# Constant rows of the shift set by GpSimd instead of VectorE, and an exponential on ScalarE ahead of the first score

## The chip, the core and the metric

The kernel runs on one core of a Trainium2 chip. The core has five engines with instruction streams of their own: TensorE (PE in the profile), VectorE (DVE), ScalarE (ACT), GpSimd (POOL) and SyncE (SP), which here does nothing but issue DMA transfers. They share an on-chip memory of 128 partitions (SBUF); TensorE writes its products into a second one (PSUM). Engines meet only at semaphores: an instruction adds to one when it is done, and another engine waits until it has a value. The metric is the device time of one execution in microseconds (us).

## What is computed

One transformer layer on a sequence of 2048 rows of 128 numbers, with 16 heads of width 64 and 8 experts of width 352 of which each row uses 2, beside a shared one:

```python
x = x + attention(layernorm(x), qkv_w, qkv_b, out_w, out_b)
    # logits = q k^T / 8, causal mask, softmax, times v, times out_w
x = x + ffn(layernorm(x), gate_w, expert_*, shared_*)
    # shared: (silu(x Wg) * (x Wu)) Wd; routed: softmax of 8 logits, top 2,
    # their weights made to sum to 1, each expert the same form
```

## The kernel before, in words

**Blocks and heads.** The 2048 rows are NB = 4 blocks of 512, or NT = 16 tiles of 128. For each of the 16 heads the scores are computed transposed (keys on partitions, queries along the row) in NG = 20 groups of two key tiles by one block of queries. A group is two score products on TensorE (`scores`, L1308 and L1309), masks for diagonal tiles (L1321), two exponentials on ScalarE (`exps`: L719 writes the value in 32 bits, L720 in 16), a subtraction on GpSimd that gives the low part (`p_low`, L585), and the product with v (`p_times_v`, L1340 to L1344), which runs LAG = 3 groups later. There are two score buffers (STRING = 2), so group n + 2 waits for the exponentials of group n.

**The shift.** Softmax needs the maximum of each query row. The maxima of a head are worked out one head ahead, by products on TensorE (L1233) that VectorE reduces (L1024 on the diagonal, L1028 elsewhere). They are negated, turned (L1238), split in two 16-bit parts divided by 16384 (L1037, L1040) and laid by DMA (L471, L476) into rows D and D + 1, that is 64 and 65, of `q_lo_shift`. The second score product, L1309, has 66 rows: rows 64 and 65 of `k_hi_one` hold the constant SHIFT_UNIT = 16384 in all 2048 columns, so that it adds the shift to every score. These constant rows, one pair for each of the two sets of buffers, are written once. Before, VectorE does it with its first two instructions (L1084), and TensorE waits for `one_rows` ahead of its first score.

**The opening.** SyncE issues x in four transfers (L417, one block each, into `attn`), then the weights. For each block VectorE takes statistics of the rows (L796, L800), ScalarE the square root of the variance (L641), VectorE the reciprocal and the normalised rows (L806, L809), TensorE turns them (L1205), ScalarE writes the 16-bit high part (L646) and VectorE the low part (L815). Then come the products for q and k of head 0 (L1198 to L1200, named `qk`), split by ScalarE (L674) and VectorE (L1009), those for v (L1223, L680, L1018), and the first maxima. The order of all of that on each engine is written out by hand in `first_norm` and the lists PROLOGUE and SLOTS. ScalarE also rounds the first weights (L705) when they have landed, and GpSimd takes the remainder (`split_pair_weights`, L544), which the first q and k product needs (`w_lo_ready`).

**GpSimd at the start** makes the constants: the identity, `eps`, the masks (L531, L534, which count `masks_ready` to 2), the columns of ones beside v (L537), the start value of the maxima (L538) and a row of whole numbers (L539). Of these, those that count `consts` are waited for by ScalarE ahead of its first exponential, and by TensorE and VectorE ahead of the first masked maximum.

**ScalarE's tables.** A function such as the square root or the exponential needs its table, which an ACT_TABLE_LOAD brings in. Copies run in either. The loads are put into the stream ahead of the first instruction that needs another table. The kernel calls a square root on one number at its start (L723), whose result nothing uses.

Of the kernel before, what the change touches and what calls it, by code (L numbers as in the profile page):

```python
# [14 lines left out]
ALU, ACT = mybir.AluOpType, mybir.ActivationFunctionType  # L15
# [7 lines left out]
H, D = 16, 64  # L23
# [9 lines left out]
SHIFT_UNIT = 16384.0  # L33
# [142 lines left out]
def layer_kernel(nc, x_t, x_rows_in, qkv_w, qk_bias_in, v_bias, out_w, out_bias, gate_w_t, ffn_w, out_rows):  # L176
    ctx = ExitStack()
    with ctx:
        def sb(name, shape, dtype):
            return ctx.enter_context(nc.sbuf_tensor(name, shape, dtype))  # L180
# [4 lines left out]
        def sem(name):  # L185
            return ctx.enter_context(nc.semaphore(name))
# [6 lines left out]
        def part(k):  # L193
            return qk_parts[:, k * T:(k + 1) * T]
# [8 lines left out]
        q_lo_shift, k_hi_one = [part(2), part(6)], [part(3), part(7)]  # L203
# [9 lines left out]
        std = sb("std", [P, NT], F32)  # L213
# [18 lines left out]
        eps = sb("eps", [P, 1], F32)  # L232
# [98 lines left out]
        consts, pool_self, masks_ready = sem("consts"), sem("pool_self"), sem("masks_ready")  # L331
        one_rows = sem("one_rows")
# [1 line left out]
        bias_sum_ready, res_bias_ready = sem("bias_sum_ready"), sem("res_bias_ready")  # L334
        x_stats, x_mean_var, ln_std, ln_rstd = sem("x_stats"), sem("x_mean_var"), sem("ln_std"), sem("ln_rstd")
        x_normalised, x_turned, xn_ready = sem("x_normalised"), sem("x_turned"), sem("xn_ready")
        sqrt_warm = sem("sqrt_warm")
        xn_hi_ready, xn_lo_ready = sem("xn_hi_ready"), sem("xn_lo_ready")
        res_ready = sem("res_ready")
        st_ready, exp_done = sem("st_ready"), sem("exp_done")  # L340
# [39 lines left out]
        def blk(b):  # L380
            return slice(b * BLK, (b + 1) * BLK)
# [139 lines left out]
        def _(pool):  # L521
# [11 lines left out]
                                    pattern=[[-1, P]], channel_multiplier=1).then_inc(masks_ready, 1)  # L533
            nc.gpsimd.affine_select(out=mask_cols[:], in_=mask_cols[:], compare_op=ALU.is_ge, fill=NEG, base=0,  # L534
                                    pattern=[[1, P]], channel_multiplier=-1).then_inc(masks_ready, 1)
            for s in range(2):
                nc.gpsimd.memset(v_parts[s][:, :, :, D:D + 1], 1.0).then_inc(consts, 1)  # L537
            nc.gpsimd.memset(row_max[:], -1.0e9).then_inc(consts, 1)  # L538
# [54 lines left out]
            for h in range(H):  # L593
                i, s = divmod(h, 2)
# [41 lines left out]
        def _(act):  # L636

            def first_norm():
                def deviation(b):
                    act.wait_ge(x_mean_var, b + 1)  # L640
                    nc.scalar.activation(std[:, 4 * b:4 * b + 4], mean_var[:, 4 * b:4 * b + 4, 1], ACT.Sqrt, bias=eps[:]  # L641
                                         ).then_inc(ln_std, 1)

                def high_part(b):
                    act.wait_ge(x_turned, b + 1)
                    nc.scalar.copy(xn_hi[:, blk(b)], turn_bank[b]).then_inc(xn_hi_ready, 1)  # L646

                def whole(b):
                    act.wait_ge(xn_lo_ready, b + 1)
                    nc.scalar.copy(xn[:, blk(b)], turn_bank[b]).then_inc(xn_ready, 1)  # L650

                deviation(0)
                deviation(1)
                split_pair_weights(0)
                high_part(0)
                deviation(2)
                high_part(1)
                deviation(3)
                qk_high(0)
                high_part(2)  # L660
                qk_high(1)
                high_part(3)
                qk_high(2)
                for b in range(NB):
                    whole(b)
                    if b == 0:
                        qk_high(3)
                split_out_weights(0)
                for q in range(4):
                    v_high(q)  # L670
            def qk_high(b):
                act.wait_ge(bg_ready, drained(("qk", 0, b)))
                act.wait_ge(w_landed[0], 32)
                nc.scalar.activation(k_lohi[0][:, blk(b)], bg[:, NUMBER["qk", 0, b] % BGRING, :], ACT.Identity,  # L674
                                     bias=qk_bias[0][:, 0:1]).then_inc(qk_hi_ready, 1)

            def v_high(q):
                act.wait_ge(bg_ready, drained(("v", 0, q)))
                bank = bg[:, NUMBER["v", 0, q] % BGRING, :]
                nc.scalar.copy(v_quad(0, q, 0, D), bank.rearrange("p (t h c) -> p h t c", t=4, h=2)).then_inc(v_hi_ready, 1)  # L680
# [22 lines left out]
            def split_pair_weights(i):  # L703
                act.wait_ge(w_landed[i % 2], (i // 2 + 1) * 32)
                nc.scalar.copy(w_hi[i % 2], w_raw[i % 2][:, :, 0:2 * D]).then_inc(w_hi_ready, 1)  # L705

            def split_out_weights(i):
                act.wait_ge(wo_landed, 32)
                nc.scalar.copy(wo_hi[i % 2], wo_all[:, i, :]).then_inc(wo_hi_ready, 1)
# [17 lines left out]
            act.wait_ge(masks_ready, 2)  # L727
            nc.scalar.copy(mask_cols_b[:], mask_cols[:]).then_inc(consts, 1)
            first_norm()
            act.wait_ge(consts, N_CONST + 2)  # L730
            for h in range(H):
                i, s = divmod(h, 2)
# [59 lines left out]
        def _(dve):  # L792
# [25 lines left out]
            def first_norm():  # L818
                x_statistics(0)
                x_statistics(1)  # L820
                normal(0)
                x_statistics(2)
                normal(1)
                low_part(0)
                x_statistics(3)
                normal(2)
                low_part(1)
                normal(3)
                low_part(2)
                low_part(3)  # L830
# [249 lines left out]
                nc.vector.tensor_tensor(attn[:, 4 * b:4 * b + 4, s * D:(s + 1) * D], pv4[:, :, 0:D],  # L1080
                                        rden[:, B % 2].broadcast_to([P, 4, D]), ALU.mult).then_inc(attn_ready, 1)

            for s in range(2):
                nc.vector.memset(k_hi_one[s][D:D + 2, :], SHIFT_UNIT).then_inc(one_rows, 1)  # L1084
            first_norm()
            for task in PROLOGUE[0:8]:
                background_task(task)
# [479 lines left out]
```

## Time and profile before

| | us |
|---|---|
| median of three runs | 918.85 (917.88 to 920.42) |
| the profiled execution, device time | 918.86 |
| its span | 917.1 |
| TensorE busy | 853.2 (93%) |
| ScalarE, VectorE, GpSimd busy | 684.9, 695.6, 710.7 |
| mean granted TensorE clock | 0.974 |

Around the span there are 918.86 - 917.1 = 1.8 us that the profile doesn't divide. A line such as `41.10 0.60 PE L1308 MATMUL st<-qk_parts ... [1.89 <-ACT p_parts L720]` reads: starts 41.10 us after the span's start, takes 0.60 us, on TensorE, line 1308 of the kernel, writes `st` from `qk_parts`; TensorE had been idle for 1.89 us until the ScalarE instruction of line 720 that writes `p_parts` ended. Buffers are shown by the tensor's name, so `k_hi_one` and `q_lo_shift`, which are pieces of `qk_parts`, carry that name; x lands in `attn`, the rounded weights are `split`, and the normalised rows stand in `prob`.

### The profile page before, as it was taken

How to read it: one execution, taken by the hardware profiler on the slowest of the kernel's cores; microseconds unless marked ns; L12 is line 12 of the kernel's file. 1: busy time of each engine (PE TensorE's matmuls, PEld its weight loads, DVE VectorE, ACT ScalarE, POOL GpSimd, SP SyncE). 2: the span in 40 equal slices, each digit the busy share in tenths (PEclk: the TensorE clock that was granted, in tenths of full speed). 3: DMA queues.
4: the chain of work that ended last, by engine and by line, in shares of the span. 5: the costliest groups of instructions: out<-in, count | busy, mean ns of one | idle time of the engine just before them, and what ended most of it. 6: DMA issues, size and time to landing. Idle time of an engine off the chain costs nothing.

```text
span 917.1 us, 25699 instructions
## 1 busy us (share of the span) xinstructions
PE 853.2 (93%) x10266; PEld 577.4 (63%) x10266; DVE 695.6 (76%) x1771; ACT 684.9 (75%) x842; POOL 710.7 (77%) x448
## 2 busy tenths in 40 slices
PE   4788999999999999999999999999999787969997
PEld 2345666666666666666666666666666563538886
DVE  7798797888879797989797979787976455445444
ACT  4366888988898889898989898988889782124442
POOL 1466889999999899889989898988889877254442
PEclk9799999999999999999999999999999999779998
DMA  6121232323242424233301020202020001112214
GB/s 181 24 52 65 56 67 65 68 55 68 64 74 50 79 55 86 64 69 73 62 17 42 16 48 1 58 2 48 2 48 3 2 2 44 40 39 69 62 44 145
DMA packets 60149, 48.33 MB, mean 53 GB/s; under 512 B 8688, under 2 KB 57714, under 8 KB 59904
## 3 DMA queue, kind: packets, MB, share of 16 engines
q1 hardware_dynamic: 57760, 42.48, 20.7%
q0 software_dynamic: 2272, 4.22, 1.3%
q8 instruction: 83, 1.36, 0.6%
q14 instruction: 34, 0.28, 0.1%
HBM read 13.93 MB, written 16.29 MB: 33 GB/s over the span
## 4 chain that ended last, share of the span: by engine, by line
PE 60%; DVE 25%; issue 5%; POOL 4%; ACT 3%; DMA 2%; SPq 1%; POOLq 0%; DVEq 0%; ACTq 0%
DVE row_max L1028 10%; PE st L1308 7%; PE st L1309 7%; PE bg L1233 7%; PE pv L1340 5%; PE pv L1342 4%; PE pv L1344 4%; POOL p_parts L585 4%; DVE junk L1024 3%; PE bg L1483 3%; PE bg L1223 3%; PE bg L1200 2%; PE bg L1198 2%; PE bg L1199 2%; DVE att_parts L1050 2%
## 5 line engine op out<-in xcount | busy, mean ns | idle before, releaser
L585 POOL TENSOR_TENSOR p_parts<-prob,p_parts 128x1024 f16<-128x1024 f32 x320 | 612.4, 1935 | 93.5 <-ACT p_parts L720 91.6
L719 ACT ACTIVATE prob<-st,p_bias 128x1024 f32<-128x1024 f32 x320 | 331.1, 1035 | 101.9 <-PE st L1309 72.3
L720 ACT ACTIVATE p_parts<-st,p_bias 128x1024 f16<-128x1024 f32 x320 | 330.8, 1034 | 0.0
L1028 DVE TENSOR_REDUCE row_max<-bg 128x1 f32<-128x512 f32 x384 | 250.6, 685 | 9.4 <-PE bg L1233 8.2
L1340 PE MATMUL pv<-v_parts,p_parts 128*128 128x65 f16 x2176 | 232.7, 193 | 3.2 <-POOL p_parts L585 2.6
L1342 PE MATMUL pv<-v_parts,p_parts 128*128 128x64 f16 x2176 | 233.0, 195 | 0.0
L1344 PE MATMUL pv<-v_parts,p_parts 128*128 128x65 f16 x2176 | 231.9, 192 | 0.0
L1308 PE MATMUL st<-qk_parts 128*128 128x512 f16 (+3 forms) x640 | 221.7, 349 | 7.4 <-ACT p_parts L720 4.6
L1309 PE MATMUL st<-qk_parts 66*128 66x512 f16 (+3 forms) x640 | 220.6, 351 | 0.0
L1340 PEld LDWEIGHTS pv<-v_parts,p_parts 128*128 128x128 f16 x2176 | 202.3, 96 | 28.4 <-DVE attn L1080 9.0
L1233 PE MATMUL bg<-qk_parts 128*128 128x512 f16 (+3 forms) x640 | 210.7, 353 | 9.8 <-DVE row_max L1028 2.1
L1342 PEld LDWEIGHTS pv<-v_parts,p_parts 128*128 128x128 f16 x2176 | 201.8, 97 | 16.0 <-issue 0.3
L1344 PEld LDWEIGHTS pv<-v_parts,p_parts 128*128 128x128 f16 x2176 | 202.2, 99 | 0.0
L1024 DVE CUSTOM_DVE_ANT_0 junk<-bg,mask_wide 128x128 bf16<-128x128 f32 (+3 forms) x256 | 121.7, 483 | 3.1 <-PE bg L1233 2.1
L1233 PEld LDWEIGHTS bg<-qk_parts 128*128 128x128 f16 x640 | 62.9, 98 | 77.4 <-DVE row_max L1028 13.1
L1309 PEld LDWEIGHTS st<-qk_parts 66*128 66x128 f16 x640 | 62.4, 97 | 52.6 <-issue 1.4
L1308 PEld LDWEIGHTS st<-qk_parts 128*128 128x128 f16 x640 | 62.9, 98 | 50.0 <-ACT p_parts L720 7.0
L1007 DVE TENSOR_SCALAR qk_parts<-bg,qk_bias 128x512 f16<-128x512 f32 x60 | 44.9, 749 | 53.8 <-PE bg L1200 53.6
L622 POOL DMA_INDIRECT y_dram<-p_parts,v_parts x39 | 37.8, 970 | 48.5 <-DVE p_parts L1159 39.1
L777 ACT ACTIVATE prob<-st 128x352 f32<-128x352 f32 x39 | 18.1, 463 | 49.7 <-PE st L1464 40.2
L1167 DVE TENSOR_TENSOR prob<-prob,st 128x352 f32<-128x352 f32 x39 | 20.3, 521 | 44.5 <-issue 37.9
L1009 DVE SCALAR_TENSOR_TENSOR qk_parts<-bg,qk_bias,qk_parts 128x512 f16<-128x512 f32 x64 | 47.9, 751 | 2.6 <-ACT qk_parts L674 0.5
(230 smaller groups left out, 1048.3 us busy)
## 6 DMA issues: line engine op xcount, KB each, us to landing
qk_parts<-qk_parts SPq DMA_DIRECT2D x192, 64.0 KB, 2.0
row_dram<-fill SPq DMA_DIRECT2D x8, 1290.0 KB, 10.6
qk_parts<-qk_parts SPq DMA_DIRECT2D x16, 256.0 KB, 3.0
stage_raw<-ffn_w SPq DMA_DIRECT2D x16, 176.0 KB, 2.6
v_parts<-row_dram SPq DMA_DIRECT2D x39, 64.5 KB
qk_parts<-y_dram SPq DMA_DIRECT2D x8, 256.0 KB, 4.7
w_raw<-qkv_w SPq DMA_DIRECT2D x8, 192.0 KB, 2.3
down_w<-ffn_w SPq DMA_DIRECT2D x1, 1536.0 KB, 8.1
```

Of the source, the lines that this page charges most:

```text
L585: nc.gpsimd.tensor_tensor(o, a, b, ALU.subtract).then_inc(p_lo_ready, 1)
L719: nc.scalar.activation(o32, src, ACT.Exp, bias=p_bias[:], scale=D ** -0.5)
L720: nc.scalar.activation(o16, src, ACT.Exp, bias=p_bias[:], scale=D ** -0.5).then_inc(exp_done, 1)
L1009: nc.vector.scalar_tensor_tensor(out=q_lo_shift[s][:, blk(b)], in0=bank, scalar=bias, in1=k_lohi[s][:, blk(b)], op0=ALU.add, op1=ALU.subtr ...
L1024: nc.vector.tensor_tensor_reduce(masked[k % BGRING][:, 0:width], bank[:, 0:width], mask_wide[:, BLK - width:BLK], 1.0, -3.0e38, ALU.add, A ...
L1028: nc.vector.tensor_reduce(row_max[:, t, c:c + 1], bank, AX_X, ALU.max).then_inc(bg_drained, 1)
L1233: mm = nc.tensor.matmul(bank[:, 0:width], q_hihi[s][:, tile(t)], k_lohi[s][:, c * BLK:c * BLK + width], start=True, stop=True)
L1308: nc.tensor.matmul(out, k_lohi[s][:, tile(kt)], q_hihi[s][:, q], start=True, stop=False)
L1309: mm = nc.tensor.matmul(out, k_hi_one[s][0:D + 2, tile(kt)], q_lo_shift[s][0:D + 2, q], start=False, stop=not diagonal)
L1340: nc.tensor.matmul(out, p_hi[:, n % PRING, cols], v[:, 0:D + 1], start=(kt == 0 and j == 0), stop=False, skip_group_check=True)
L1342: nc.tensor.matmul(out[:, 0:D], p_hi[:, n % PRING, cols], v[:, D + 1:VW], start=False, stop=False, skip_group_check=True)
L1344: mm = nc.tensor.matmul(out, p_lo[:, n % PRING, cols], v[:, 0:D + 1], start=False, stop=(kt == 4 * b + j), skip_group_check=True)
```

## The change

GpSimd writes the constant rows, between the masks and the columns of ones, with one wait ahead (for its own masks) and one behind; VectorE no longer does. ScalarE calls an exponential on one number, into a cell of `std` that has been read by then, when its work of the opening is issued, and waits for it ahead of its first score.

```diff
-        sqrt_warm = sem("sqrt_warm")
+        sqrt_warm, exp_warm = sem("sqrt_warm"), sem("exp_warm")
@@ gpsimd
             nc.gpsimd.affine_select(out=mask_cols[:], in_=mask_cols[:], compare_op=ALU.is_ge, fill=NEG, base=0,
                                     pattern=[[1, P]], channel_multiplier=-1).then_inc(masks_ready, 1)
+            pool.wait_ge(masks_ready, 2)
+            for s in range(2):
+                nc.gpsimd.memset(k_hi_one[s][D:D + 2, :], SHIFT_UNIT).then_inc(one_rows, 1)
+            pool.wait_ge(one_rows, 2)
             for s in range(2):
                 nc.gpsimd.memset(v_parts[s][:, :, :, D:D + 1], 1.0).then_inc(consts, 1)
@@ scalar
             first_norm()
+            nc.scalar.activation(std[:, 1:2], eps[:], ACT.Exp).then_inc(exp_warm, 1)
+            act.wait_ge(exp_warm, 1)
             act.wait_ge(consts, N_CONST + 2)
@@ vector
-            for s in range(2):
-                nc.vector.memset(k_hi_one[s][D:D + 2, :], SHIFT_UNIT).then_inc(one_rows, 1)
             first_norm()
```

On GpSimd, from the masks to the remainder of the first weights (`split`), the order before is:

```order
L534 AFFINE_SELECT mask_cols<-mask_cols 128x128
L537 MEMSET v_parts 128x32 x2
L538 MEMSET row_max 128x64
L539 IOTA iota_row 128x128
L544 TENSOR_TENSOR split<-w_raw,split 128x256
```

and after the change, whose file has other line numbers:

```order
L534 AFFINE_SELECT mask_cols<-mask_cols 128x128
L538 MEMSET qk_parts 2x2048 x2
L541 MEMSET v_parts 128x32 x2
L542 MEMSET row_max 128x64
L543 IOTA iota_row 128x128
L548 TENSOR_TENSOR split<-w_raw,split 128x256
```

Two MEMSETs of 2 partitions by 2048 numbers now stand ahead of five instructions, the last of which TensorE waits for. On ScalarE, from the last copy of the normalised rows to the second exponential of the first group, the order before is:

```order
L709 CAST split<-wo_all 128x128
L680 CAST v_parts<-bg 128x2x4x64 x4
L719 ACT_TABLE_LOAD
L719 ACTIVATE prob<-st,p_bias 128x1024
L720 ACTIVATE p_parts<-st,p_bias 128x1024
```

and after:

```order
L713 CAST split<-wo_all 128x128
L684 CAST v_parts<-bg 128x2x4x64 x4
L734 ACT_TABLE_LOAD
L734 ACTIVATE std<-eps 128x1
L723 ACTIVATE prob<-st,p_bias 128x1024
L724 ACTIVATE p_parts<-st,p_bias 128x1024
```

The table load now belongs to the exponential on one number, which waits for no other engine; the first exponential of the scores has none of its own.

## Rows read from the trace of the kernel before

**Rows 1.** The page's first line: the span.
```profile
span 917.1 us, 25699 instructions
```

**Rows 2.** The chain that ended last, in order of time: start, us, what.
```profile
1.30 1.76 DVE qk_parts L1084
...
5.24 0.88 DVE stats L796 x4
...
37.60 0.03 issue
37.63 1.28 ACT L719
38.93 1.11 ACT prob L719
...
67.90 6.72 DMA qk_parts<-shift_row
```

**Rows 3.** Issues of x, and us from issue to landing of blocks 0, 1, 2.
```profile
0.81 2.11 SPq L417 DMA_DIRECT2D attn<-x_rows_in  x4
...
DMA to landing us min/median/max: 3.0/3.0/3.0
...
DMA to landing us min/median/max: 3.3/3.3/3.3
...
DMA to landing us min/median/max: 5.1/5.1/5.1
```

**Rows 4.** VectorE in order of time, opening: start, us, instruction, xcount.
```profile
6.44 0.84 DVE L796 BATCH_NORM_STATS2 stats<-attn 128x6 f32<-128x128 f32 x4
...
7.79 1.11 DVE L809 TENSOR_SCALAR prob<-attn,mean_var,rstd 128x128 f32<-128x128 f32 x4
8.82 0.87 DVE L796 BATCH_NORM_STATS2 stats<-attn 128x6 f32<-128x128 f32 x4
...
11.23 0.68 DVE L815 TENSOR_TENSOR xn_lo<-st,xn_hi 128x512 f16<-128x512 f32 x1
```

**Rows 5.** ScalarE in order of time, opening; brackets: idle before, and its releaser.
```profile
8.68 0.40 ACT L705 CAST split<-w_raw 128x256 f16<-128x256 f32 x1 [0.65 <-DMA qk_bias<-qk_bias_in]
10.17 0.59 ACT L646 CAST xn_hi<-st 128x512 f16<-128x512 f32 x1 [1.09 <-PE st L1205]
...
37.63 1.28 ACT L719 ACT_TABLE_LOAD   x1 [11.65 <-PE st L1321]
```

**Rows 6.** GpSimd in order of time, then groups by shape (busy us, mean ns), then L537.
```profile
2.85 0.38 POOL L537 MEMSET v_parts<- 128x32 f16 x2
...
3.12 0.28 POOL L539 IOTA iota_row<- 128x128 f32 x1
9.16 0.67 POOL L544 TENSOR_TENSOR split<-w_raw,split 128x256 f16<-128x256 f32 x1 [5.76 <-ACT split L705]
...
L556 POOL TENSOR_SCALAR res<-res,res_bias 128x2048 f32<-128x2048 f32 x1 | 5.4, 5447 | 4.1 <-DVE res_bias L1090 4.1
L528 POOL MEMSET mask_wide<- 128x512 f32 x1 | 0.5, 514 | 0.0
L526 POOL MEMSET eps<- 128x1 f32 x1 | 0.1, 88 | 0.0
...
L537 POOL MEMSET v_parts<- x2: 238/281/324, 2.9 to 2.9; 128x32 f16 x2
```

**Rows 7.** TensorE and VectorE around head 0's third group; then stretch 42 to 43.
```profile
12.28 0.63 PE L1198 MATMUL bg<-xn_hi,split 128*128 128x512 f16 x1
...
41.10 0.60 PE L1308 MATMUL st<-qk_parts 128*128 128x512 f16 x1 [1.89 <-ACT p_parts L720]
...
42.59 0.69 DVE L1028 TENSOR_REDUCE row_max<-bg 128x1 f32<-128x512 f32 x1 [2.28 <-PE bg L1233]
...
44.69 0.38 PE L1233 MATMUL bg<-qk_parts 128*128 128x512 f16 x1
...
42.00:43.00 1.00, 1.00 (x4) 0.37 (x3) 0.41 (x1) 0.20 (x1) 1.00 (x1) 0.50 0.00 0
```

In the last row the numbers are: length of the stretch, busy us and count of TensorE, its weight loads, VectorE, ScalarE and GpSimd, granted clock as a share of full speed, DMA share and GB/s.

## The prediction

> **What bounds the kernel now.** I read the chain of waits in order of time first. The span is 917.1 us [rows 1], and both instructions that the change touches are links of that chain [rows 2]: it opens on VectorE with two MEMSETs of 1.76 us, the first at 1.30, runs on to the statistics of x at 5.24, and passes through ScalarE's table load, 1.28 us at 37.63, to the first exponential at 38.93. The reader is to see that these links come before everything else: the opening is one chain of short steps across VectorE, TensorE and ScalarE, with no slack of its own. Then I read the landing of x, since the statistics wait for that too; then ScalarE, GpSimd and VectorE in order of time in the first 12 us, for what would be late next; and TensorE with its granted clock around the first scores. Behind 75 us nothing changes: sixteen heads, the routing and the experts follow in the same order, so what matters is only how much earlier they begin.
>
> **Term 1, the MEMSETs leave VectorE.** The statistics of block 0 start at 5.24 [rows 2]. With the MEMSETs gone they wait for x alone. Its first transfer is issued at 0.81 and lands 3.0 us later, at 3.8 [rows 3]. Counting a landing from the start of its issue, and 0.06 us (an estimate, from gaps such as the 0.03 of issue in [rows 2]) to the waiting instruction, the statistics start at 3.87. The gain is 5.24 - 3.87 = 1.37 us, not the 3.94 us from 1.30 to 5.24: two thirds of the removed time was beside the transfer anyway.
>
> What is late next? The other blocks of x: the four issues take 2.11 us from 0.81, about 0.53 apart [rows 3]. Block 1 lands at 1.33 + 3.3 = 4.6; its statistics would start at 6.44 - 1.37 = 5.07 [rows 4]. Block 2 lands at 1.87 + 5.1 = 7.0; it is wanted at 8.82 - 1.37 = 7.45 [rows 4]. Both are there with about 0.45 us to spare. ScalarE: the rounding of the weights stands at 8.68 because the weights' bias lands then [rows 5], and this does not move. Behind it stands the high part of block 0, now at 10.17, which could start at 8.80 but gets its turn at 9.08. It ends at 9.08 + 0.59 = 9.67. VectorE takes it up at 11.23 now [rows 4], or 9.86 then, as its own work stands ahead. So the 0.28 us are hidden. I take the whole 1.37; the bounds are 0.9 (x or the weights a little late) and 1.6.
>
> **Term 2, the MEMSETs come to GpSimd.** No row shows a MEMSET of 2048 numbers there. The nearest ones are contiguous fills: 1 number 88 ns, 512 numbers 514 ns [rows 6], so 0.834 ns for each further number, and 88 + 2047 x 0.834 = 1.79 us for one, 3.6 for two, from about 2.95 (where the columns of ones start now, 2.85, and 0.1 for the wait on the masks). What stands behind them, from the columns of ones at 2.85 to the end of the row of numbers at 3.12 + 0.28 = 3.40, takes 0.55 us more, so GpSimd is free at 7.1. Its next work, the remainder of the weights, is released at 9.16 by ScalarE [rows 6]: cost 0, covered by 2.0 us of idle time. The others who wait for these constants do so after 26 us. Upper bounds: at the rate of the 128x2048 operation, 5.45 us each, GpSimd would be free at 2.95 + 10.9 + 0.55 = 14.4, the remainder done at 15.1, and the first q and k product, now at 12.28 [rows 7], would be 2.8 us late. At the rate of the 32-number fill of v_parts, (238 - 88) / 31 = 4.8 ns [rows 6], one takes 9.9 us, GpSimd is free at 23.3, the remainder done at 24.0, and the product 11.7 us late. I take 1.79, since the fill of v_parts differs in its stride and the 128x2048 row reads as well as writes.
>
> A rule speaks mildly against this half of the change. Beside the second MEMSET VectorE would begin the normalised rows (L809, at 7.79 - 1.37 = 6.4 [rows 4]). The Trainium skill (SBUF — State Buffer, Who interferes with whom) says that a VectorE tensor_scalar in a two-port mode and GpSimd lock each other out for a whole instruction. By that rule VectorE would wait until about 6.6, and the time would be 0.2 us longer; no row shows GpSimd filling beside such an instruction, and the sum goes without it.
>
> **Term 3, the table load.** ScalarE is idle for 11.65 us ahead of the load [rows 5]: it has nothing to do between the last of v's high parts, which ends at 37.63 - 11.65 = 26.0, and the first score. The load and the exponential on one number fit there with some 10 us to spare, and cost nothing. The load is removed from between the mask product and the first exponential: 38.93 - 37.63 = 1.30 us [rows 2]. TensorE's third group waits for these exponentials, with 1.89 us of idle time [rows 7], and VectorE waits 2.28 us for the product of a maximum behind that group [rows 7], so both engines move by the whole 1.30 and neither has other work that would be in the way: bounds 1.0 and 1.3. From there the chain is mostly VectorE's maxima up to 67, the end of head 0's last shift, then its transfer, which takes 6.72 us at 67.90 behind a large load of weights [rows 2]. Both are issued by SyncE in the same order and after work of VectorE, so they move with the rest.
>
> The Trainium skill (ScalarE: Activation LUTs, What ACT_TABLE_LOAD costs) puts a switch of tables at about 2.66 us, 1.28 for the load and 1.38 for a drain. The 1.28 agrees with the trace. The drain is not in it: 0.03 us of issue stand between the mask product, for which ScalarE waited, and the load, and 0.02 us between the load's end and the exponential [rows 2, 5]. By the rule the sum would be 1.38 us lower.
>
> **Sum.** 918.86 (the profiled execution) - 1.37 + 0 - 1.30 = 916.19. The median of the runs shown is 918.85, so nothing has to be converted. That is 0.29% faster; a change of 0.3% (2.8 us) is about what a measurement of this kernel can tell from none, and the three runs before span 2.5 us.
>
> **TensorE's clock** is the unknown of the opening. From 41.10 to 44.69 its products of 512 columns take 0.63 us, later 0.38 [rows 7]; the granted clock in between is 0.50 of full speed [rows 7], the lower of the two levels, 1.2 GHz. It fell after the idle time in front of 41.10 that waited for ScalarE. With the load gone this idle time is 1.89 - 1.30 = 0.6 us, and the clock may stay at 2.4 GHz. The stretch of 3.6 us at half rate would take 1.8 less, but VectorE has six maxima of up to 0.69 us there [rows 7], 3 to 4 us of work of its own, so I estimate 1.0 more gained, at most 1.8. It can go the other way too: if the clock rises at the same time after the start as now and not at the same place in the work, 1.37 us more of TensorE's work runs at half rate in the opening (12.28 is such a place, 0.63 us for 512 columns [rows 7]), and each such rise gives back up to 1.37 / 2 = 0.7 us. There is at least one more than the one at 44.69, since the clock that fell at 41 had been up.
>
> **The rivals.**
> - *Clean shift*, 916.2, give or take 0.6. For it: every wait behind the two links follows from them. Chance 0.45.
> - *The clock stays up at 41 us*, 915.2. For it: the shorter idle time. Against it: 0.6 us of it is left, and ScalarE, not TensorE, sets the pace of the next groups. Chance 0.22.
> - *Part is given back*, at the clock's rises, by the lock of the SBUF port, or by x landing late in a stretch where transfers share the engines: one of the terms halves, 917.2 to 918.0. Chance 0.22.
> - *The drain exists*, hidden from the rows: 916.19 - 1.38 = 914.8. Against it: the two gaps of 0.03 and 0.02 us [rows 2]. Chance 0.03.
> - *GpSimd's fill is slow, and the first q and k product waits for the remainder of the weights.* At the upper rate 11.7 us late instead of 1.37 early: 918.86 + 11.7 - 1.30 = 929.3. It decides where two MEMSETs hold GpSimd beyond 12.28 + 1.30 - 0.67 - 0.55 = 12.4 us, that is at over 4.7 us each, where the time is 918.86 again; at 5.45 us it is 918.86 + 2.8 - 1.3 = 920.4. For it: the shape is in no row, and GpSimd's v_parts fill is slow. Chance 0.04, with 0.04 more for a slowdown that I can't name.
>
> **How the numbers follow.** The predicted time is the clean shift's, 916.2. The limit of 0.3% is at 916.1, so half of the clean shift's chance is on either side of it. Faster by over 0.3%: 0.23 + 0.22 + 0.03 + 0.01 of the third case = 0.49. Within: 0.22 + 0.21 = 0.43. Slower: 0.08. The range of 8 in 10 leaves out the slow fill and the ends: 914.2, the clock with its upper gain, to 918.7, where nearly all is given back.
>
> **What would show it.** In the profile of the changed kernel the statistics of block 0 start at 3.9 with x's transfer as the releaser; GpSimd's two MEMSETs take 1.8 us each and its remainder of the weights still starts at about 9.2; the first q and k product is at 10.9; ScalarE has a table load at about 25 and none at the first score; the first exponential starts at 38.93 - 2.67 = 36.3, and TensorE's first product of head 0's last block, now behind the transfer that ends at 74.6 [rows 2], at about 72.0. The prediction is wrong if the MEMSETs last over 4 us, if the first exponential moves by less than 2 us, or if it moves by 2.7 us and the end does not.

## The result, and the profile after

The changed kernel took 914.50 us, median of 7 runs (912.64 to 917.08), against 918.23 us for the kernel before (7 runs, 915.92 to 920.42). The ratio is 0.9960, 95% interval 0.9942 to 0.9978: 3.7 us faster, between 2.0 and 5.3. Forecast were 2.7. On another chip the ratio was 0.9975 (0.9965 to 0.9985): 895.12 us, median of 9 runs, against 896.98, median of 17, so 2.2 us by the ratio, between 1.3 and 3.1. Both intervals hold the forecast.

The chain that ended last, in order of time (start, us, what), of the changed kernel; it answers to [rows 2]:

```profile
0.79 3.04 DMA attn<-x_rows_in
3.86 0.88 DVE stats L802 x4
...
63.99 6.66 DMA qk_parts<-shift_row
...
70.79 0.38 PE st L1312
```

The MEMSETs of VectorE are gone, and x's transfer stands in their place: the statistics start at 3.86, forecast 3.87. The transfer of head 0's last shift starts at 63.99 instead of 67.90, 3.9 us earlier, where 2.67 were forecast. VectorE in order of time in the opening, which answers to [rows 4]:

```profile
6.41 1.33 DVE L815 TENSOR_SCALAR prob<-attn,mean_var,rstd 128x128 f32<-128x128 f32 x4
7.67 0.86 DVE L802 BATCH_NORM_STATS2 stats<-attn 128x6 f32<-128x128 f32 x4
...
9.04 1.19 DVE L815 TENSOR_SCALAR prob<-attn,mean_var,rstd 128x128 f32<-128x128 f32 x4
10.15 0.68 DVE L821 TENSOR_TENSOR xn_lo<-st,xn_hi 128x512 f16<-128x512 f32 x1
```

The first four normalised rows take 1.33 us instead of 1.11, the next four 1.19 instead of 1.12. So the low part of block 0 (the last line) starts 11.23 - 10.15 = 1.08 us earlier, and not 1.37. GpSimd and then ScalarE of the same kernel; they answer to [rows 6] and [rows 5]:

```profile
2.94 3.54 POOL L538 MEMSET qk_parts<- 2x2048 f16 x2
...
8.71 0.67 POOL L548 TENSOR_TENSOR split<-w_raw,split 128x256 f16<-128x256 f32 x1 [1.62 <-ACT split L709]
```

```profile
24.43 0.60 ACT L684 CAST v_parts<-bg 128x512 f16<-128x512 f32 x1 [0.99 <-PE bg L1227]
25.04 1.28 ACT L734 ACT_TABLE_LOAD   x1
26.33 0.20 ACT L734 ACTIVATE std<-eps 128x1 f32<-128x1 f32 x1
36.65 1.11 ACT L723 ACTIVATE prob<-st,p_bias 128x1024 f32<-128x1024 f32 x1 [10.12 <-PE st L1325]
```

The two MEMSETs take 1.77 us each (forecast 1.79), and GpSimd still waits 1.62 us for ScalarE behind them. The table load stands where ScalarE has nothing else to do; 10.12 us of idle time are left behind it. The first exponential starts at 36.65 instead of 38.93, 2.28 us earlier, where 2.67 were forecast. So 0.4 us had been lost by then: some 0.29 at the normalised rows and 0.12 at the last block of x, which TensorE turned in 0.94 us before and in 1.06 us now. And between the first exponential and 64 us 3.91 - 2.28 = 1.6 us more were gained. TensorE of the changed kernel at the third group, with the granted clock (third number from the end) of three stretches; they answer to [rows 7]:

```profile
38.25 0.63 PE L1237 MATMUL bg<-qk_parts 128*128 128x512 f16 x1
38.83 0.45 PE L1312 MATMUL st<-qk_parts 128*128 128x512 f16 x1
39.12 0.38 PE L1313 MATMUL st<-qk_parts 66*128 66x512 f16 x1
```

```profile
38.00:39.00 1.00, 1.00 (x6) 0.39 (x4) 0.96 (x4) 1.00 (x2) 0.15 (x1) 0.51 0.00 0
39.00:40.00 1.00, 1.00 (x6) 0.40 (x5) 0.86 (x2) 0.93 (x2) 1.00 (x1) 1.00 0.00 0
...
42.00:43.00 1.00, 0.47 (x16) 0.35 (x12) 0.94 (x4) 1.00 (x2) 0.72 (x2) 1.00 0.00 0
```

Here the clock rises to full speed just before 39 and stays. In the profile of before it was at half from 41 to 44.7. The forecast had named that as a rival, with "at most 1.8 us". The experiments ask whether the change brought it about.

### The profile page after: what moved, and what is told of

Its sections match the earlier page's. It is cut to its first block, busy times and chain, and to the rows that moved or that the text cites. A ratio compares the mean times of both kernels' runs of the same rounds, so it can differ in the third digit from the quotient of the medians.

```text
span 912.8 us, 25700 instructions
## 1 busy us (share of the span) xinstructions
PE 851.0 (93%) x10266; PEld 576.5 (63%) x10266; DVE 692.0 (76%) x1769; ACT 685.1 (75%) x843; POOL 714.1 (78%) x450
## 4 chain that ended last, share of the span: by engine, by line
PE 59%; DVE 24%; POOL 4%; issue 4%; DMA 3%; ACT 3%; another core or an unknown queue 2%; SPq 1%; POOLq 0%; DVEq 0%; ACTq 0%
DVE row_max L1034 10%; PE st L1312 7%; PE st L1313 7%; PE bg L1237 7%; PE pv L1344 5%; PE pv L1346 5%; PE pv L1348 4%; POOL p_parts L589 4%; DVE junk L1030 3%; PE bg L1487 3%; PE bg L1227 3%; PE bg L1204 2%; PE bg L1202 2%; PE bg L1203 2%
```

## The experiments

Theory A: the two parts add up, and beside them the table load's idle time on TensorE made the clock fall, so that its going keeps the clock up. Theory B, the rival: the idle time has no part in it; the phase of the clock against the work decides, and only 2.5 us belong to the change.

The runs of this section are from three other chips, on which the kernel before takes about 897 us. A profile shows one execution; where a time is given as a ratio, it is from six to ten runs of the kernel named, against 23 (first three experiments) or 17 runs of the kernel before on the same chip. The opening is nearly the same on all: the statistics of the kernel before start at 5.24 there too.

**The MEMSETs alone moved.** The edit, against the changed kernel:

```diff
-            nc.scalar.activation(std[:, 1:2], eps[:], ACT.Exp).then_inc(exp_warm, 1)
-            act.wait_ge(exp_warm, 1)
```

> The changed kernel without its exponential on one number: only the MEMSETs move to GpSimd. Theory A (the two parts are separate, and the clock stayed up because the table load no longer makes TensorE idle): statistics of block 0 start at 3.86 instead of 5.24; the first exponential, behind its table load, starts 1.0 us earlier than before (37.9); TensorE's idle time ahead of the third group stays about 1.9 us and the clock falls there as before, so TensorE's first product of the last block of head 0 comes at about 73.8 (74.76 - 1.0) and the time is about 1.0 us under before. Theory B (the clock's phase against the start of the kernel decides, not the idle time): the clock stays up here too, and that product comes at 72.3, time 2.4 us under before.

Measured: ratio to before 1.0001 (0.9990 to 1.0012), 897.42 against 897.37 us. ScalarE and TensorE in order of time:

```profile
36.47 1.28 ACT L723 ACT_TABLE_LOAD   x1 [11.65 <-PE st L1323]
37.77 1.11 ACT L723 ACTIVATE prob<-st,p_bias 128x1024 f32<-128x1024 f32 x1
...
39.94 0.61 PE L1310 MATMUL st<-qk_parts 128*128 128x512 f16 x1 [1.89 <-ACT p_parts L724]
40.34 0.63 PE L1311 MATMUL st<-qk_parts 66*128 66x512 f16 x1
```

and of its chain that ended last:

```profile
66.78 6.72 DMA qk_parts<-shift_row
...
73.64 0.38 PE st L1310
```

The first exponential is 1.16 us earlier than in the first profile of before, the clock falls at 40 (the product of 512 columns takes 0.63), and TensorE's first product of head 0's last block came at 73.64, forecast 73.8. As to the opening this was theory A's numbers. But the time did not move: the interval reaches 0.9 us down, so that the 1.0 us expected here lies a little outside it, and the 1.37 us of the prediction's first term further.

**The exponential alone added.** The edit, against the changed kernel:

```diff
@@ gpsimd
-            pool.wait_ge(masks_ready, 2)
-            for s in range(2):
-                nc.gpsimd.memset(k_hi_one[s][D:D + 2, :], SHIFT_UNIT).then_inc(one_rows, 1)
-            pool.wait_ge(one_rows, 2)
@@ vector
+            for s in range(2):
+                nc.vector.memset(k_hi_one[s][D:D + 2, :], SHIFT_UNIT).then_inc(one_rows, 1)
             first_norm()
```

> The changed kernel with its MEMSETs back on VectorE: only the exponential on one number is added. Theory A: the statistics start at 5.24, the first exponential at 37.6 (1.30 earlier), TensorE's idle time ahead of the third group is 0.6 us, the clock does not fall there, and the first product of the last block of head 0 comes at 74.76 - 1.3 - 1.4 = 72.0; time 2.7 us under before. Theory B: the opening has its old phase, the clock falls as before; the product comes at 73.5, time 1.3 us under before.

Measured: ratio 0.9969 (0.9951 to 0.9986), 895.29 against 897.37 us. The first exponential starts at 37.80, the clock stays up from 40 on, the first product of the last block comes at 71.58 (forecast 72.0). Theory A's numbers again, and here the time agrees too (2.8 us, between 1.3 and 4.4; 2.7 expected). Theory B's 1.3 is at the edge of the interval.

**The kernel before, with TensorE kept busy in the gap.** The edit, against the kernel before, in `scores`, ahead of its first wait:

```diff
+                if h == 0 and n == 2 and k == 0:
+                    for _ in range(7):
+                        nc.tensor.matmul(pv[:, :], xn_hi[:, 0:P], xn_hi[:, blk(0)], start=True, stop=True)
```

> The kernel before with seven more products of 128x512 on TensorE (into the bank of the v products, which is free then), issued ahead of the wait of the third group of head 0, where TensorE is idle for 1.9 us; the table load stays where it was. Theory A: TensorE has no idle time there, the granted clock stays at full speed through 41 to 45, the maxima end 1.4 us earlier, and the first product of the last block comes at about 73.4, time 1.4 us under before. Theory B (idle time does not matter): the clock falls at 41 as before, the product stays at 74.7 and the time is unchanged.

Measured: ratio 0.9985 (0.9973 to 0.9996), 896.37 us, 1.3 us by the ratio, between 0.4 and 2.4 (1.4 expected). The clock stays up, the last shift's transfer starts at 66.48, 1.42 us earlier than in the first profile of before. That looked like a proof of theory A, and the next repetition took the profile's part of it away.

**The kernel before, unchanged, profiled again.** It was run beside the kernels that follow, and then three times more on another chip.

> The kernel before, profiled on the chip of this comparison, so that openings can be laid beside each other. Both theories: its opening repeats to 0.2 us (statistics 5.24, first exponential 38.9, first product of head 0's last block 74.8), since in the runs so far the opening hardly depended on the chip. If that product moves by over 0.5 us between two executions of this kernel, single looks at the opening can't tell theories apart.

Measured: the expectation fell. The statistics are at 5.24 and the first exponential at 39.04, but the product of the last block came at 72.71, 2.05 us earlier than in the first profile, over four times the 0.5 us beyond which single profiles of the opening can't tell the theories apart. TensorE in order of time at the third group, and then the chain's transfer:

```profile
39.17 0.42 PE L1321 MATMUL st<-mask_cols_b,ident_b 128*128 128x128 bf16 x2
41.22 0.39 PE L1308 MATMUL st<-qk_parts 128*128 128x512 f16 x1 [1.20 <-ACT p_parts L720]
```

```profile
66.57 6.00 DMA qk_parts<-shift_row
```

Without any edit the product behind the gap takes 0.39 us and not 0.60: the clock is up, and the transfer starts at 66.57, where the kernel with the seven fills had 66.48. So the profile with the fills had shown nothing. Its time is lower all the same: the interval doesn't hold 1. Whether the fills help in those executions in which the clock would fall is not shown.

> The kernel before, unchanged, a third profile. The question is how often TensorE's clock falls in front of the third group of head 0. So far: in the first profile of this kernel and in the one with the MEMSETs alone moved it rose at 37.4 (36.2) and fell at 41 (40); in the second profile of this kernel it rose only at about 39 and did not fall, which moved the last shift's transfer from 67.90 to 66.57. Theory A' (the table load's idle time makes a fall possible, and the phase of the clock decides whether it comes): some of these three profiles show the fall, with the transfer at 67.9, the others show none, with 66.5. Theory C (the first profile was an outlier): none does.

> The same kernel again, as the run ahead of it. Theory A': fall or none, transfer of the last shift at 67.9 or at 66.5 and nothing in between. Theory C: no fall, 66.5.

> The same kernel again, as the two runs ahead of it. Theory A': fall or none, transfer of the last shift at 67.9 or at 66.5. Theory C: no fall, 66.5.

Measured: none of the three shows a fall, which is theory C's forecast. First exponential at 39.40, 39.05 and 39.05; the transfer starts at 66.95, 66.54 and 66.35. Of five profiles of the kernel before, the first alone has it, and beside it the one with the MEMSETs alone moved. In these two the clock rose early, at about 37.7 and 36.6 by the shares of the stretches of 1 us (0.63 in 37 to 38, 0.72 in 36 to 37), and fell behind the gap. In the other four profiles of the kernel before it rose between 39.2 and 40.1 and stayed. (The expectation of the third profile put the two rises 0.3 us too early.) The two patterns part much earlier, at the products for the third block's q and k. Here is the first of them in the first and in the second profile of the kernel before:

```profile
17.34 0.38 PE L1198 MATMUL bg<-xn_hi,split 128*128 128x512 f16 x1
```

```profile
17.41 0.63 PE L1198 MATMUL bg<-xn_hi,split 128*128 128x512 f16 x1
```

The third to fifth profiles have 0.63 or 0.64 there too, and the kernel with the MEMSETs alone moved has 0.38, at 16.18. What sets the moment of the first rise no run shows.

The third profile's exponential is 0.35 us late for another reason. VectorE and then GpSimd:

```profile
7.79 1.47 DVE L809 TENSOR_SCALAR prob<-attn,mean_var,rstd 128x128 f32<-128x128 f32 x4
```

```profile
8.46 0.71 POOL L544 TENSOR_TENSOR split<-w_raw,split 128x256 f16<-128x256 f32 x1 [5.06 <-ACT split L705]
```

ScalarE rounded the weights early in this execution, at 7.97 instead of 8.68, and GpSimd's subtraction of them ran beside the normalised rows, which took 1.47 us instead of 1.11.

So the first profile is one outcome of two, and the rarer. Against the common one, 39.05 and 66.5, the kernel with the MEMSETs alone moved gains 1.28 us at the first exponential (37.77), of which 0.12 belong to the early clock, and then loses it to the clock (66.78 is no earlier than 66.5). That agrees with its ratio of 1.0001, as far as one profile can say; but ten runs were timed, and that the clock fell in most of them is not shown.

**The changed kernel again.**

> The changed kernel once more, timed in five rounds on the chip of this comparison. Theory A (two parts that add up, and the clock that stays up): first product of head 0's last block 3.9 us earlier than in the kernel before (70.8), time 3.9 us under it, ratio 0.9957. Theory B (the clock's part was luck of one execution): 2.5 us, ratio 0.9973, with the clock at half speed somewhere between 39 and 45.

> The changed kernel, a third profile. In its two profiles so far the clock rose at 38.2 to 38.8 and stayed up, with the transfer at 64.0 and 64.1. Theory A': with 0.6 us of idle time no fall comes whatever the phase, transfer at 64.0 again. Theory C says the same. If it falls here, the transfer is at about 65.4 and the change has no bearing on the clock.

Measured, the first of them timed: ratio 0.9975 (0.9965 to 0.9985). ScalarE's first exponential and the chain's transfer:

```profile
36.63 1.11 ACT L723 ACTIVATE prob<-st,p_bias 128x1024 f32<-128x1024 f32 x1 [10.17 <-PE st L1325]
```

```profile
64.07 6.77 DMA qk_parts<-shift_row
```

Against the profile of the kernel before on the same chip that is 39.04 - 36.63 = 2.41 us at the exponential and 66.57 - 64.07 = 2.50 at the transfer's start. The 2.2 us of the timing (1.3 to 3.1) agree with that and not with theory A's 3.9. It is theory B's forecast of 2.5 that came out, though not by its mechanism, since the clock was never at half between 39 and 45. The forecasts were for TensorE's first product of the last block, though, and that starts at 70.98 against 72.71, 1.73 us earlier and not 2.5: the transfer ahead of it took 6.77 us here and 6.00 there. The third profile started its first exponential at 37.60 and the transfer at 65.05, 1.0 us later than the other two. TensorE in order of time shows where most of the difference arose:

```profile
18.95 0.58 PE L1202 MATMUL bg<-xn_hi,split 128*128 128x512 f16 x1 [0.87 <-DVE qk_parts L1015]
19.33 0.63 PE L1203 MATMUL bg<-xn_lo,split 128*128 128x512 f16 x1
19.75 0.63 PE L1204 MATMUL bg<-xn_hi,split 128*128 128x512 f16 x1
```

These are the products for the last block's q and k; in the other two profiles each took 0.38 us. TensorE reached full speed later in the work, and by the end of v's products it was 25.11 - 24.15 = 0.96 us behind. Of that, 0.33 us had been there ahead of these products: the normalised rows of block 1 took 1.45 us instead of 1.11, beside GpSimd's subtraction (8.97 to 9.64), and VectorE's last low part starts at 17.45 instead of 17.12. The clock's share is 0.6.

Behind the transfer this profile shows something that none of the theories has. The granted clock is at half again, from about 73.6 for 3.4 us. First a stretch of it and the eight products for v of that time, then the same products in the second profile of the changed kernel:

```profile
74.00:75.00 1.00, 1.00 (x18) 0.94 (x17) 1.00 (x4) 1.00 (x2) 0.00 (x0) 0.50 0.00 0
...
75.38 1.90 PE L1227 MATMUL bg<-w_raw,xn 128*128 128x128 f32 x8
```

```profile
73.54 1.13 PE L1227 MATMUL bg<-w_raw,xn 128*128 128x128 f32 x8
```

VectorE's next scaling of the products with v by the row sums (L1086, in the kernel before L1080) starts at 82.94, against 80.33 and 80.15 in the other two profiles, and 82.06 to 82.78 in the last four profiles of the kernel before: at this point nothing is left of the gain. The kernel with the MEMSETs late, below, shows the same (73.6, scaling at 82.81). The last such scaling, at the end of head 15, starts at 757.39 and 758.25 in the second and third profiles of the changed kernel and at 758.96 to 759.49 in those four, 0.7 to 2.1 us later.

**The MEMSETs three times.** The edit, against the changed kernel:

```diff
-            for s in range(2):
-                nc.gpsimd.memset(k_hi_one[s][D:D + 2, :], SHIFT_UNIT).then_inc(one_rows, 1)
-            pool.wait_ge(one_rows, 2)
+            for k in range(6):
+                if k > 1:
+                    pool.wait_ge(one_rows, k - 1)
+                nc.gpsimd.memset(k_hi_one[k % 2][D:D + 2, :], SHIFT_UNIT).then_inc(one_rows, 1)
+            pool.wait_ge(one_rows, 6)
```

with TensorE's wait for `one_rows` raised to 6.

> The changed kernel with each constant-row MEMSET issued three times on GpSimd (six of 1.77 us, from 2.9 to about 13.9 with the waits between them). GpSimd's remainder of the first weights then starts at about 14.4 instead of 8.7 and ends at 15.1. If it is covered by idle time only up to the first q and k product, as predicted, that product starts at 15.1 instead of 11.2, and everything behind it, the first exponential too, is 3.9 us later than in the changed kernel (40.5). Rival (other work hides part of it): less than 2 us later.

Measured: VectorE, GpSimd and TensorE in order of time:

```profile
2.95 10.96 POOL L540 MEMSET qk_parts<- 2x2048 f16 x6
...
6.35 3.93 DVE L817 TENSOR_SCALAR prob<-attn,mean_var,rstd 128x128 f32<-128x128 f32 x4
...
11.56 2.50 DVE L817 TENSOR_SCALAR prob<-attn,mean_var,rstd 128x128 f32<-128x128 f32 x4
14.52 0.66 POOL L550 TENSOR_TENSOR split<-w_raw,split 128x256 f16<-128x256 f32 x1
15.33 0.58 PE L1204 MATMUL bg<-xn_hi,split 128*128 128x512 f16 x1
```

The remainder of the weights starts at 14.52 and the product at 15.33; forecast were 14.4 and 15.1. The first exponential came at 40.16, 3.5 us later than in the changed kernel, 3.9 forecast. So the point from which the MEMSETs delay the first product is where the prediction had put it. But there is a second effect that it had left out of the sum: VectorE's four normalised rows take 3.93 us instead of 1.11 beside the fills, and the next four 2.50. The statistics between them (0.85 for four) are not lengthened at all. One kind of VectorE instruction stands still while GpSimd fills, the other runs on. The chain that ended last goes over this second effect and not over the first product:

```profile
11.56 2.50 DVE prob L817 x4
14.06 0.59 DVE xn_lo L823
```

VectorE's low part of block 0 starts at 13.98, 3.83 us later than in the changed kernel, and the product 4.13 us later. The two are so close that this run doesn't show what the delayed product alone would have cost. One time only was taken, 899.03 us.

**The MEMSETs late.** The edit, against the changed kernel: the MEMSETs and their waits move from behind the masks to

```diff
             split_out_weights(0)
+            pool.wait_ge(wo_lo_ready, 1)
+            for s in range(2):
+                nc.gpsimd.memset(k_hi_one[s][D:D + 2, :], SHIFT_UNIT).then_inc(one_rows, 1)
+            pool.wait_ge(one_rows, 2)
             pool.wait_ge(res_bias_ready, 1)
```

> The changed kernel with its two MEMSETs on GpSimd behind the remainder of the first output weights, in the idle time between 22.4 and 26.4, where VectorE works from the other memory. If GpSimd's fill holds back VectorE's normalised rows (the first tensor_scalar took 760 ns beside it, 347 before), the first four now take 1.11 us instead of 1.33 and the first exponential comes 0.2 to 0.3 us earlier than in the changed kernel (36.4); time 0.3 us less, which the timing can't tell. Rival: the lengthening came from x's transfers, and the four stay at 1.33. A risk: the fill ends at 26.0 and the addition to the residual starts at 26.4, so nothing is late.

Measured: ratio 0.9970 (0.9959 to 0.9981), 894.92 us, beside 0.9975 of the changed kernel: no difference that can be told. VectorE and GpSimd:

```profile
6.49 1.11 DVE L815 TENSOR_SCALAR prob<-attn,mean_var,rstd 128x128 f32<-128x128 f32 x4
...
8.69 0.67 POOL L544 TENSOR_TENSOR split<-w_raw,split 128x256 f16<-128x256 f32 x1 [5.29 <-ACT split L709]
...
8.90 1.30 DVE L815 TENSOR_SCALAR prob<-attn,mean_var,rstd 128x128 f32<-128x128 f32 x4
```

The first four are back at 1.11, so it was GpSimd's work that lengthened them, the fills or the short constants that had been behind them, and not x's transfers. The next four now take 1.30: they meet GpSimd's remainder of the weights, from 8.69 to 9.36, which in the first profile of the kernel before lay between two such groups. So the low part starts at 10.13, no earlier than the changed kernel's 10.07 and 10.15. The first exponential came at 37.31, not at 36.4, for the same reason as in the changed kernel's third profile: the last q and k products were at half rate. The 0.2 us that the edit gives at the first rows are smaller than what the subtraction and the clock do by themselves.

**The MEMSETs late, and TensorE kept at work.** The edit, against the kernel just told of, with two more products of 128x512 ahead of the third group:

```diff
             pe.wait_ge(ones_ready, 1)
+            for _ in range(20):
+                nc.tensor.transpose(pv[:, 0:P], ident[:], ident[:])
             turn_normal(0)
...
-            for task in PROLOGUE[8:]:
+            for k, task in enumerate(PROLOGUE[8:]):
+                if k == 3:
+                    pe.wait_ge(res_bias_ready, 1)
                 background_task(task)
+                if k >= 3:
+                    nc.tensor.matmul(pv[:, :], xn_hi[:, 0:P], xn_hi[:, blk(0)], start=True, stop=True)
...
-            pe.wait_ge(res_bias_ready, 1)
```

> The previous kernel (MEMSETs late) with idle TensorE kept at work in the opening: 20 turns of the identity before the first normalised rows, one product of 128x512 behind each maximum of the prologue from the fourth on, and two ahead of the third group, all into the bank of the v products. If the clock is the other lever of the opening, granted clock 1.0 from about 10 to 45, products of 512 columns at 0.38 us throughout, the first exponential about 2 us earlier than without (34.4), and 1 more us by the end of the first maxima of the next groups; time 2.5 to 3 us under the changed kernel, ratio to before 0.993. Rival: the opening is bound by VectorE, and the fills gain under 1 us.

Measured: ratio 0.9962 (0.9950 to 0.9975), 894.19 us. TensorE, then ScalarE's first exponential and the chain's transfer:

```profile
10.88 0.63 PE L1202 MATMUL bg<-xn_hi,split 128*128 128x512 f16 x1
...
18.37 0.38 PE L1202 MATMUL bg<-xn_hi,split 128*128 128x512 f16 x1 [0.87 <-DVE qk_parts L1015]
...
33.20 0.38 PE L1315 MATMUL st<-qk_parts 128*128 128x512 f16 x1
...
34.85 1.11 ACT L723 ACTIVATE prob<-st,p_bias 128x1024 f32<-128x1024 f32 x1 [8.64 <-PE st L1328]
```

```profile
62.26 6.50 DMA qk_parts<-shift_row
```

The 20 turns at the start had no effect: the products from 10.88 to 17 still took 0.63 us. The fills between the maxima did: the first scores, from 33.20, take 0.38 where they took 0.63 in the changed kernel, and the first exponential comes at 34.85 (34.4 expected), 1.8 us earlier than the changed kernel's 36.63. The transfer starts 1.8 us earlier too. But the median is only 0.9 us under the changed kernel's, where 2.5 to 3 were expected, and the intervals of the two ratios overlap, so that this version has the lowest ratio but is not clearly the fastest. The same profile shows where part of the gain went: the clock is at half from 69.2 for 3.4 us, the first product of the last block takes 0.56 us instead of 0.38, and the next scaling (L1086) starts at 79.71, only 0.62 us ahead of the changed kernel's 80.33.

## Why the prediction was right, and where it was not

- **The MEMSETs leave VectorE.** Right in the profiles: 5.24 became 3.86 by the row; x's transfer is what ends the wait; blocks 1 and 2 were in time. Not shown in the time: the MEMSETs alone moved gave a ratio of 1.0001, and the 1.37 us of this term lie outside its interval.
- **The MEMSETs come to GpSimd at no cost.** Their size (1.77 for 1.79) and their cover (GpSimd idle behind them) were right. The cost was not zero: they hold VectorE's normalised rows back by 0.19 to 0.27 us. The prediction had set this aside as a rule of the Trainium skill (SBUF — State Buffer, Who interferes with whom) that no row showed. The traces agree with the rule and its 0.2 us: in the four profiles with the MEMSETs there these rows start at 6.37 to 6.45 and all end at 7.74 or 7.75, as if all had begun at about 6.6; beside six fills they take 3.93 us, with the fills elsewhere 1.11. By the same section a VectorE instruction with one input outside the two-port modes is free of it, and the statistics were.
- **The weights.** The prediction took it that ScalarE's rounding stands at 8.68 and does not move. It starts between 7.97 and 8.68 in the five profiles of the kernel before, and where GpSimd's subtraction behind it meets normalised rows, these take longer, by 0.07 us (first profile of the changed kernel, block 1) to 0.36 us (third profile of the kernel before, block 0). So this cost comes without the change too; by its earlier rows the change only moves where it can fall.
- **The table load.** Right. In the kernel with the exponential alone added, the first exponential came at 37.80 against 39.04 to 39.05 in three of the five profiles of before, 1.25 us; the load's row is 1.28. No drain was seen: the load starts 0.01 us after a copy has ended and the exponential on one number 0.01 us after the load. The 2.66 us that the Trainium skill gives (ScalarE: Activation LUTs, What ACT_TABLE_LOAD costs) are not what a switch takes here.
- **The sum.** 2.67 forecast; 2.41 at the first exponential and 2.50 at the transfer by two profiles of one chip, 2.2 (1.3 to 3.1) by its timing. Of the 0.26 missing at the exponential 0.19 is the hold-up of the normalised rows beside GpSimd. At the product behind the transfer the same two profiles have 1.73. So the sum is good to 0.4 us at the first exponential in two profiles, and 1.2 us off in the third; the two halves add up there (1.16 without the early clock, and 1.25, against 2.41) but are not told apart by the times (the MEMSETs alone moved: between 1.1 us slower and 0.9 faster; the exponential alone added: between 1.3 and 4.4 faster).
- **The clock.** The rival in which the clock stays up described the pair of profiles that the prediction started from, with 1.4 us for its "1.0, at most 1.8". As a mechanism of this change it is not shown. The kernel before does the same without the change in four profiles of five. The step that failed was to read a feature of one execution, half speed from 41 to 44.7, as a property of the kernel. The case in which part is given back is real as well: in the changed kernel's third profile the clock took 0.6 us in the opening and the subtraction 0.3. Its first exponential, 37.60, is only 1.45 us ahead of its chip's 39.05, less than the 2 us that the prediction had named as a sign of being wrong.
- **Behind 75 us** the prediction saw nothing but the same work, earlier. Three of the seven profiles with the exponential issued early (the changed kernel's third, and the two with the MEMSETs late) show the clock at half for 3.4 us in head 0's last block, from 73.6 or 69.2, and none of the seven with the load in place does. Whether the change brings this about is open.
- **The first comparison's 3.7 us.** Its interval reaches down to 2.0, and its profiles differ by 3.9 at 64 us, of which some 1.4 are the clock's. Whether on that chip the kernel before takes the early rise more often than elsewhere, or the median was merely lucky, stays open.
- **Also open:** whether the shorter gap protects against the fall at 41. None of the seven profiles in which the exponential is issued early shows it; but only two of the seven with the load in place do, which is too few to tell.

## What to carry to other kernels

A table load, or any work that waits for nothing, belongs in idle time of its engine, and what it gives can be read off as the gap between its row and the next. An instruction moved from VectorE to GpSimd is not free because GpSimd is idle: look at what VectorE runs meanwhile, and whether it is of the kind that stands still beside a fill. And before a stretch at half clock is priced, the same kernel should be profiled a second time: a difference of 1 to 1.4 us between two profiles of this opening needed no edit at all. A gain at the start should be followed to the end, too: here one profile in three had none of it left at 83 us.

## What the runs showed of the hardware

- VectorE's tensor_scalar of 128x128 in 32 bits stands still while GpSimd fills: beside back-to-back fills of 1.83 us apiece (10.96 for six), four of them took 3.93 us instead of 1.11. Statistics (four in 0.85 to 0.87) did not. Beside GpSimd's subtraction of 128x256 (0.67 to 0.71 us) four such rows took 1.19 to 1.47 us.
- A fill of 2 partitions by 2048 16-bit numbers takes GpSimd 1.77 us and took VectorE 1.76: for this shape the two engines fill at the same rate.
- Over its first 26 us the granted clock reads 1.00 in every profile, while products of 512 columns take 0.63 us until about 16 to 20 us, as they do where it reads 0.50. There the duration of a product tells more than the clock's row, and 20 turns of the identity, from 1.6 to 6.1 us, did not raise the rate of the products from 10.88 to 17.
- The transfer of 1 KB behind the 1.5 MB load of weights took 6.0 to 7.1 us in fourteen profiles, and 6.00 to 6.80 in the five of the kernel before; that alone is up to 0.8 us between two executions of one kernel.
- In the middle of head 0's scores the granted clock fell to half for 3.4 us, at 40 to 41 or at 69 to 74 us, in five of fourteen profiles, and in one of the changed kernel's three the whole gain was gone by the next scaling (82.94 us against 80.33).
